# The entropy model of a fused attention kernel in another order: two steps of one side together, and a first tanh over 2048 columns

## The reference

```
# x: (8, 192, 64, 64) float32; gn: group norm over 32 groups
x = x + attention(gn(x))        # q, k: 24 channels, v: 192 channels, each 1x1 conv + prelu; softmax over 4096 positions
x = x + likelihood(gn(x))

def logits_cumulative(logits, ms, bs, fs):            # per channel, widths 1, 3, 3, 3, 1
    for i in range(4):
        logits = einsum('cij,cjn->cin', softplus(ms[i]), logits) + bs[i]
        if i < 3:
            logits = logits + tanh(fs[i]) * tanh(logits)
    return logits
def likelihood(x):
    lower = logits_cumulative(x - 0.5, ...)
    upper = logits_cumulative(x + 0.5, ...)
    sign = -sign(lower + upper)
    return maximum(abs(sigmoid(sign * upper) - sigmoid(sign * lower)), 1e-6)
```

## Time and profile before

| | |
|---|---|
| median of 3 runs | 4760.89 us (4754.21 to 4761.35) |
| the profiled execution's own time | 4754.35 us |
| its span | 4752.5 us |
| PE busy | 4428.2 us, 93% |
| DVE busy | 4099.3 us, 86% |
| ACT busy | 3736.5 us, 79% |
| mean granted TensorE clock | 0.984 |
| DMA, share of 16 engines | 21.4% (the SP queue) |

### The profile page before, as it was taken

How to read it: one execution, slowest core, us unless ns; L and a number is a source line. 1 busy time by engine, 2 the same in 40 slices (tenths; PEclk the granted TensorE clock), 3 DMA queues, 4 the chain that set the end, 5 groups by cost and what they waited for, 6 DMA issues and landing times.

```text
span 4752.5 us, 108300 instructions
## 1 busy us (share of the span) xinstructions
PE 4428.2 (93%) x38780; PEld 2977.4 (63%) x38780; DVE 4099.3 (86%) x5433; ACT 3736.5 (79%) x4214; POOL 813.8 (17%) x937
## 2 busy tenths in 40 slices
PE   5999989999899999999899998999989999899976
PEld 3888338873488735887258862688617885278821
DVE  6997899978999789996999969999698987999866
ACT  2777788868888698886988869787797877978787
POOL 4100201202022110211111120121201212022112
PEclk9999999999999999999999999999999999999998
DMA  2000321114211142111411124110331112311133
GB/s 68 25 21 25 97 73 53 38 39 100 68 51 36 44 103 62 46 44 40 111 51 53 36 58 104 40 61 28 78 89 49 47 41 75 93 49 34 40 93 94
DMA packets 155019, 280.19 MB, mean 59 GB/s; under 512 B 37441, under 2 KB 37921, under 8 KB 152706
## 3 DMA queue, kind: packets, MB, share of 16 engines
q1 hardware_dynamic: 154434, 272.69, 21.4%
HBM read 205.24 MB, written 50.33 MB: 54 GB/s over the span
## 4 chain that ended last, share of the span: by engine, by line
PE 72%; ACT 11%; DVE 7%; issue 7%; DMA 0%; ACTq 0%; POOL 0%; DVEq 0%; POOLq 0%
PE ps L1514 14%; PE ps L1512 14%; PE ps L1516 13%; PE ps L1288 9%; PE ps L1465 8%; ACT th L799 5%; ACT arena L792 4%; PE ps L1387 3%; PE ps L1321 3%; DVE th L1123 3%; PE ps L1373 3%; PE ps L1345 2%; DVE mxp L1191 2%; PE ps L1296 1%; PE ps L1280 1%
## 5 line engine op out<-in xcount | busy, mean ns | idle before, releaser
L1514 PE MATMUL ps<-v_sb,arena 128*128 128x192 f16 x8192 | 2026.8, 247 | 0.0
L1512 PE MATMUL ps<-v_sb,arena 128*128 128x193 f16 x8192 | 2017.9, 246 | 0.0
L1516 PE MATMUL ps<-v_sb,arena 128*128 128x193 f16 x8192 | 2009.9, 245 | 0.0
L755 ACT ACTIVATE arena<-ps 128x1024 f16<-128x1024 f32 x1024 | 1049.0, 1024 | 644.5 <-PE ps L1288 640.7
L1083 DVE TENSOR_TENSOR arena<-ps,arena 128x1024 f16<-128x1024 f32 x1024 | 1245.6, 1217 | 166.8 <-ACT ps L756 158.5
L1191 DVE TENSOR_REDUCE mxp<-ps 128x1 f32<-128x512 f32 x1792 | 1191.0, 688 | 41.3 <-PE ps L1465 29.3
L1123 DVE SCALAR_TENSOR_TENSOR th<-th,gates,ps 128x1024 f32<-128x1024 f32 x768 | 950.3, 1277 | 147.2 <-ACT th L799 140.1
L756 ACT ACTIVATE ps<-ps 128x1024 f32<-128x1024 f32 x1024 | 1044.4, 1020 | 0.0
L1514 PEld LDWEIGHTS ps<-v_sb,arena 128*128 128x128 f16 x8192 | 795.1, 97 | 262.7 <-issue 0.6
L799 ACT ACTIVATE th<-ps,biases 128x1024 f32<-128x1024 f32 x768 | 825.6, 1120 | 118.5 <-PE ps L1373 80.8
L1512 PEld LDWEIGHTS ps<-v_sb,arena 128*128 128x128 f16 x8192 | 792.1, 97 | 126.3 <-issue 10.8
(11 more groups left out here) (147 smaller groups left out, 3449.8 us busy)
## 6 DMA issues: line engine op xcount, KB each, us to landing
x<-x2d SPq DMA_DIRECT2D x1152, 64.0 KB, 2.3
arena<-x2d SPq DMA_DIRECT2D x768, 64.0 KB, 2.5
xp<-x_dram SPq DMA_DIRECT2D x18, 1536.0 KB, 10.1
shared<-x_dram SPq DMA_DIRECT2D x64, 384.0 KB, 3.9
x2d<-shared SPq DMA_DIRECT2D x64, 384.0 KB, 3.0
res<-x2d SPq DMA_DIRECT2D x96, 256.0 KB
out_dram<-res SPq DMA_DIRECT2D x96, 256.0 KB
kst<-shared SPq DMA_DIRECT2D x32, 256.0 KB, 3.2
```

What stands on the lines that cost most here:

```text
L755: act.activation(e_hi[:, q % 4, :].rearrange("p (k n) -> p k n", k=2), sc, ACT.Exp)
L1512: pe.matmul(acc, eh, v_sb[:, m, 0:C + 1], start=(m == 0 and t % 2 == 0), stop=False, skip_group_check=True)
L1514: pe.matmul(acc[:, 0:C], eh, v_sb[:, m, VW:VW + C], start=False, stop=False, skip_group_check=True)
L1516: ins = pe.matmul(acc, el, v_sb[:, m, 0:C + 1], start=False, stop=(m == MT - 1), skip_group_check=True)
```

## The change

Steps are ordered by side. Step c now has side d = c // 2 % 2, so a pair of steps w (HALVES, 24 in an image) is a whole unit's 4096 positions of one side: u = w // 2, d = w % 2. Each engine takes a pair at a time:

- PE: first layer of 2w, one piece of side work, first layer of 2w + 1, third layer of pair w - 1 (one side only, four matmuls and one PSUM bank), second layer of 2w, another piece of side work, second layer of 2w + 1. Side work is value bank V_LEAD + 2w + i, or maximum 2 (w - 6) + i.
- ACT: the two tanh of the first layer, the first tanh of pair w + 2, the two tanh of the second layer, then the Relu of value banks V_LEAD + 2w and + 1.
- DVE: a reduction, the two gates of the first layer, the logits of pair w - 1, a reduction, the two gates of the second layer, then the two value instructions.

The first tanh of a pair is one instruction over 2048 columns (for the first pair it stays in pieces). x4 has two slots of a whole unit; a unit is loaded by six DMAs of 128 KB, and the first two units in halves. The side rows are loaded by two DMAs of 128 KB for a pair. t0 keeps its three tiles, th1 has four, th2 two. The wait of the first tanh is for both halves of its unit. The diff also brings weights w3f and w3h, which would take the second gate over into the third layer's matmuls for steps that are `folded`; FOLD is (False, False), so no step is, and every gate is left to DVE.

```diff
-X4R, T0R, HR1, HR2, XR, LUR = 3, 3, 2, 5, 4, 6
-LEAD = 4
-SPLIT = 1
+X4R, T0R, HR1, HR2, XR, LUR = 2, 3, 4, 2, 4, 6
+X4_DMAS = SIDES * (UNITS // X4R + 1)
+FOLD = (False, False)
...
-FIRST_AT = VB - V_LEAD + 1
+FIRST_AT = (VB - V_LEAD + 1) // 2
...
     uses = []
+    for w in range(HALVES + 1):
+        if w < HALVES:
+            uses += [("h1", 2 * w), ("h1", 2 * w + 1)]
+        if w >= 1:
+            uses.append(("h3", w - 1))
+        if w < HALVES:
+            uses += [("h2", 2 * w), ("h2", 2 * w + 1)]
...
+            def load_side(row, w):
+                for a in (1, 0):
+                    sp.dma_start(t0[64 * a + 48:64 * a + 64, w % T0R, :, :].rearrange("p d (k n) -> p (d k) n", n=N),
+                                 whole(row, w // 2, a)).then_inc(side_in[w % T0R], 16)
...
-                    load_side(l, row, 0)
                     store_x2(l, row, BLOCKS - 1)
                     for s in range(2):
                         sp.wait_ge(x2_stored[s], l * 64 + 64)
-                    load_x4(row, 1)
+                    load_side(row, 0)
+                    for u in range(X4R):
+                        load_half(row, 2 * u + 1)
...
+            pool.memset(w3f[:, :, :], 0.0)
+            pool.memset(w3h[:, :, :], 0.0)
...
+                def first_tanh(w, half=None):
+                    u, d = w // 2, w % 2
+                    if d == 0 and half != 1:
+                        loaded = 2 * SIDES + u // X4R * SIDES
+                        act.wait_ge(x4_in[u % X4R], l * X4_DMAS * 16 + loaded * 16)
+                    if w >= T0R:
+                        act.wait_ge(h1_mm, l * SLOTS + 2 * (w - T0R) + 2)
+                    if half is None:
+                        act.activation(t0[:, w % T0R, :, :], x4[:, u % X4R, :].rearrange("p (d n) -> p d n", d=2),
+                                       ACT.Tanh, bias=biases[:, d, 0, u:u + 1], scale=scl[:, u:u + 1]
+                                       ).then_inc(t0_ready, 2)
...
+                for w in range(HALVES + (0 if proj else 3)):
+                    if w < HALVES:
+                        for c in (2 * w, 2 * w + 1):
+                            if c >= HR1:
+                                act.wait_ge(h3_mm, l * HALVES + w - 1)
+                            tanh("h1", c, th1[:, c % HR1, :, :], 1, h1_mm, t1_ready)
+                    if w + 2 < HALVES:
+                        first_tanh(w + 2)
...
+                    if w < HALVES:
+                        for c in (2 * w, 2 * w + 1):
+                            if c >= HR2:
+                                act.wait_ge(h3_mm, l * HALVES + w)
+                            tanh("h2", c, th2[:, c % HR2, :, :], 2, h2_mm, t2_ready)
...
+                    for i in range(2):
+                        v = V_LEAD + 2 * w + i
+                        if proj and v < VB:
+                            negative(QK + v)
...
+                for w in range(HALVES + (0 if proj else 3)):
+                    m = 2 * (w - FIRST_AT)
+                    if proj and 0 <= m < MAXES:
+                        first_reduce(m)
...
+                    if w < HALVES:
+                        for c in (2 * w, 2 * w + 1):
+                            gate("h1", c, th1[:, c % HR1, :, :], F1O, t1_ready, h1_ready)
+                    if 1 <= w <= HALVES:
+                        logits(l, w - 1, not proj)
+                    if proj and 0 <= m < MAXES:
+                        first_reduce(m + 1)
...
+                            if not folded(c):
+                                gate("h2", c, th2[:, c % HR2, :, :], F2O, t2_ready, h2_ready)
+                    for i in range(2):
+                        v = V_LEAD + 2 * w + i
+                        if proj and v < VB:
+                            value(QK + v)
...
+                def side_work(w, i):
+                    v, m = V_LEAD + 2 * w + i, 2 * (w - FIRST_AT) + i
+                    if proj and v < VB:
+                        value_bank(v)
+                    if proj and 0 <= m < MAXES:
+                        first_max(m)
+                    if proj and m == MAXES + 1:
+                        turn_max(pj(BLOCKS, 0), 0)
+
+                for w in range(HALVES + (0 if proj else 1)):
+                    if w < HALVES:
+                        first_layer(2 * w)
+                        side_work(w, 0)
+                        first_layer(2 * w + 1)
+                    if w >= 1:
+                        third_layer(l, w - 1)
+                    if w < HALVES:
+                        if proj and w == HALVES - 1:
+                            pe.wait_ge(max_in, pj(BLOCKS * 16, 16))
+                            scores(0, 0)
+                        second_layer(2 * w)
+                        side_work(w, 1)
+                        second_layer(2 * w + 1)
```

More of the change, by code:

```diff
@@ L38 @@
 STACK_DMAS = 5
-X4_DMAS = 2 * 3
-SIDE_DMAS = 2 * 2
+SIDES = 2 * 3
+SIDE_DMAS = 2
 NORM_DMAS, CONST_DMAS = 3, 6
@@ L125, in max_tiles, with folded, unfolded_before @@
     return list(range(min(PER_STEP * p, MAXES), min(PER_STEP * (p + 1), MAXES)))
+def folded(c):
+    return FOLD[c // 2 % 2]
+def unfolded_before(c):
+    return sum(not folded(i) for i in range(c))
 def tail_unit(i, last):
@@ L209, in program @@
         w3 = sb("w3", [P, UNITS, 2 * UC])
+        w3f = sb("w3f", [P, UNITS, 2 * UC])
+        w3h = sb("w3h", [P, UNITS, 2 * UC])
         gates = sb("gates", [P, UNITS, NF])
@@ L247, in program @@
         place = [0]
-        second = th2.rearrange("p s d n -> p (s d n)")
+        first = th1.rearrange("p s d n -> p (s d n)")
         def setup_area(*shape):
@@ L481, in phase_b @@
                         sp.wait_ge(x_sums, summed_up)
-                        for v in (0, 2):
-                            load_x4(row, v)
+                        for u in range(X4R):
+                            load_half(row, 2 * u)
                     if j + 1 < BLOCKS:
@@ L573, in coefficients @@
                     spread(w2, i, 1, msp[:, :, M2C + i])
+                setup(pool.tensor_tensor(u1[:, :, 0], msp[:, :, M3C], gates[:, :, F2O], ALU.mult))
+                dot(u1[:, :, 1], [(msp[:, :, M3 + i], msp[:, :, M2C + i]) for i in range(HID)])
                 for a in range(2):
-                    ins = spread(w3, a, 2 + a, msp[:, :, M3C])
+                    spread(w3, a, 2 + a, msp[:, :, M3C])
+                    spread(w3f, a, 2 + a, u1[:, :, 0])
+                    ins = spread(w3h, a, 2 + a, u1[:, :, 1])
                 ins.then_inc(set_gp, 1)
@@ L1188, in phase_b @@
+                if proj:
+                    low(pj(BLOCKS * PAIRS, 0), 0)
             def phase_b(b, l):
```

248 lines of the change are left out of this document (106 added, 142 removed).

## The result

The changed kernel takes 4945.64 us (median of 4 runs, 4934.94 to 4950.15), the one before 4759.53 beside it: 1.039 times as long, interval 1.0371 to 1.0409. The forecast was 4890 us, slower. The direction was right, and the time lies 0.6 us above the top of the range, 4945. The profiled execution took 4934.94 us, with a mean granted clock of 0.972 against 0.984 before; it is the lowest of the four. Against the profiled execution before (4754.35) it is 181 us more, where the sum had 138.

The account below looks back on a forecast made before the run. PE, ACT and DVE were taken as nearly full, so order counts too. Seven images lose 14.6 + 2.6 + 4.3 = 21.5 us each, the last gains 12: 4754 + 138 = 4892, said as 4890; range 4825 to 4945.

Parts of the forecast that it names:

- The ring: Value stage: PE stands at V for the value two banks before; 10.13 us a pair, stage 15.6 us longer.
- rival (c): Faster: ACT's wide tanh carries the value stage, bound by ACT, and DVE the maxima; 4703 us, chance 0.07.
- The clock: PE at half clock behind some of the new stalls: 4.3 us an image, between none and 10.2.
- (a): Rival: each stall of PE brings the low clock, 10.2 us an image; 4934 us, chance 0.15.
- The maxima: Stage with the 32 maxima: 110.6 us against 110.36, so 0.2 us an image lost.
- The new ring: Maxima: chain from reduction through G1a, P2a, second maximum, P2b, T2b, G2b to reduction; 6.82 us a pair against 6.90.
- The last stage: Behind the maxima, to the first product with V: one gate less, 1.2 us an image gained.
- The head: Start of each image: first F 2.3 us late, waiting for both halves, plus Relu delay; 2.6 us an image lost.
- The last image: No banks or maxima, ACT sets the pace: 1.15 us less for each of 12 units; 12 us gained in all.
- The sum: Whole kernel: seven images lose 21.5 us each, the last gains 12; 4754 + 138 = 4892, said as 4890.

Follow-up runs that it names:

- e1: Changed kernel with the first Relu and value instruction of a pair moved between its first and second layer; 4819.22 us, 1.0129 times the kernel before.
- e10: Kernel before the change, with each value bank issued right behind the step's first layer instead of at the step's end; 4958.21 us, 1.0421.
- e7: Changed kernel with the first value bank of pairs 1 to 5 issued ahead of the pair's first first-layer group instead of behind it; 5030.83 us, 1.0574.
- e2: Changed kernel with 22 small extra matmuls on PE ahead of the banks of pairs 1 to 5 and the first maximum; 4913.33 us, 1.033.
- e5: Changed kernel with the first tanh's parts each waiting for their own input half, unit 0's second half issued ahead of side loads; 4902.79 us, 1.03.
- e8: Changed kernel with four edits: value work earlier, second maximum ahead of P2a, separate half semaphores, head Relus in old order; 4763.05 us, 1.0014.
- e3: Changed kernel with the second maximum of a pair issued on PE ahead of P2a instead of between P2a and P2b; 4916.05 us, 1.0333.

## Why the prediction was off in size

**The ring: right.** V is released by DVE's value instruction, PE idles 2.28 us before it (forecast 2.2), and a pair has 10.26 us (10.13). The difference is in three distances between PE's groups, 1.02, 1.00 and 1.01 where the forecast had 0.97, 0.93 and 0.97; for the second it had called the sixteen matmuls of its row eight, but halved their time rightly. e1 takes the wait away and the stage falls by 14.4 us, e10 plants it in the old kernel, e7 makes it longer. Free of the low clock the stage is 60.57 us, 16.1 more than before (15.6 forecast). Of these, 11.7 are the wait; the other 4.4, which e1 keeps, are PE's (a dearer first pair above all), and stood in the ring's terms unseen: rival (c), a stage set by ACT, would have failed without the wait too.

**The clock: right in kind, too high in this stage.** 2.7 us an image there (e2) against 4.3. Of the rivals, (a) asked for all six stalls; one to four spells were seen in an image, in a program that repeats itself. Of the four runs, which span 15 us, the shortest has the highest mean granted clock (0.972) and the longest the lowest (0.968). e10 and e7, with 22 and 23 us an image at half clock, show how near the rival was.

**The maxima: mis-sized.** The sum had 0.2 us and 3.1 were measured. The ring has 6.92 us, not 6.82. From the rows of the changed kernel,

```profile
1206.90 1.27 DVE L1159 SCALAR_TENSOR_TENSOR th<-th,gates,ps 128x1024 f32<-128x1024 f32 x1
...
1208.32 1.09 PE L1445 MATMUL ps<-th,w 64*64 64x512 f32 x8 [0.72 <-DVE th L1159]
1209.34 0.39 PE L1414 MATMUL ps<-kst,qst 128*128 128x512 f16 x1
1209.66 1.09 PE L1445 MATMUL ps<-th,w 64*64 64x512 f32 x8
...
1209.53 1.11 ACT L830 ACTIVATE th<-ps,biases 128x1024 f32<-128x1024 f32 x1
1210.88 2.12 ACT L830 ACTIVATE th<-ps,biases 128x1024 f32<-128x1024 f32 x2 [0.24 <-PE ps L1445]
```

P2b to T2b is 1.22 (1209.66 to 1210.88), not 1.16, and G1a (1206.90) to P2a 1.42, not 1.38: 0.1 us in each of fifteen pairs. Pair 6 was left 5.8 us and takes 7.56 (e2); the reduction and split, at 2.5, add 1.0 to the last pair. With the maxima of e1, where neither a wait nor the half clock enters, the stage is 111.74, 1.65 above before; the M that waits for the last value adds 0.65 (112.39 in e2) and the half clock 0.8. The forecast compared its ring with 110.36, a stage with 3.4 us at half clock, and not with the 109.61 of three others. It also took 110.36 / 16 = 6.90 us for two steps of before, which has the wait of the first M in it. Late in that stage four steps, from gate to gate, took 13.54:

```profile
649.49 2.47 DVE L1123 SCALAR_TENSOR_TENSOR th<-th,gates,ps 128x1024 f32<-128x1024 f32 x2
...
663.03 2.47 DVE L1123 SCALAR_TENSOR_TENSOR th<-th,gates,ps 128x1024 f32<-128x1024 f32 x2
```

That is 6.77 us for two. The new ring, forecast to be 0.08 us shorter than the old pace, is 0.15 longer in each pair.

**The last stage: -0.1 instead of -1.2.** In four images it takes 15.4 to 15.5 us (-0.7), in the three others, with 5 us of it at half clock, 17.0 to 17.1. Where the other 0.5 us of the forecast went in the four is open.

**The head: the step that failed.** The sum had 2.6 us an image, 5.5 were measured. F is 2.6 us late where 2.3 were forecast, but by two errors that nearly cancel: eight issues take 5.03 us (1092.20 to the end of the sixth half at 1097.23) and not 3.6, since the price of a 64 KB issue (0.45) was taken for the side loads of 128 KB, and in this image they begin 3.55 us ahead of the statistics (1095.75), where the row of before has 1067.99 - 1.10 - 1064.45 = 2.44. What was wrong was the rest. Behind F the forecast had 0.85 us for a Relu behind the wide F and some 0.5 us taken back, since DVE and PE waited there anyway. The Relus' place costs about what it was given: 0.7 us, from e5 to e8. But nothing is taken back: a late F costs 1.8 us more than its own lateness (22.58 us from F to the first gate, and 20.79 in e5). PE's wait at the value bank is 2.83 us instead of 1.53, and 6.0 us of the stretch lie at half clock instead of 3.5; how the 1.8 divides between the two, no run shows. Together 0.3 (ahead of the statistics) + 2.6 + 1.8 + 0.7 are the head's 5.5.

**The last image: right in sum, in part by luck.** 11.4 us gained, 12 forecast. One unit has

```profile
4776.40:4790.82 14.42, 10.77 (x84) 2.37 (x80) 11.73 (x11) 14.20 (x14) 3.83 (x4) 1.00 0.77 112
```

14.42 us with ACT busy 14.20, where it had 15.36 and 14.75: 0.94 us less, 1.15 forecast. The earlier trace rows By stages, the head of that image loses 3.8 us (2.2 forecast), the stretch from the first gate to the 45th gains 8.2 (eleven units, 12.7 forecast), and the stretch behind it gains 7.0 (33.9 us before, 26.9 after), where the forecast had one unit's 1.15. That last gain stood in no term, and nothing here explains it.

**The sum.** Per image the terms are off by +2.9 (head), +2.9 (maxima), +1.1 (last stage), +0.5 (ring) and -1.6 (clock): 5.8, times seven 41 us. The profiled execution is besides 10.7 us below the median of its runs, and the one before 5 below its own: from run to run the time moves by as much as a term. The range ended 11 us above rival (a), 4934 us, which has every stall at half clock but no error in the head or the maxima.

## What to carry to other kernels

Where a rotating buffer is freed by the last instruction of the step before, its next use must not stand at the front of an in-order queue: measure the distance from the freeing instruction to the use in the queue, in instructions and not in buffers. One bank placed a few groups sooner, with the same work and the same buffers, cost the old kernel 4%; the freeing instruction moved ahead of two gates gave the new one back 2.5%. When steps are made twice as large, price the start of each stage anew: the first large load has to be issued and landed whole before the first large instruction, and a late start can cost more than its own lateness (2.6 us late, 4.4 us lost).

## What the runs showed of the hardware

- Six DMAs of 128 KB behind one another take 4.23 us of SP's queue, 0.70 each, where those of 64 KB take 0.45 to 0.475; two side loads of 128 KB at the head of the second image held it for 2.18 us. The 128 KB land after 4.8 us (3.8 for side rows) where 64 KB land after 2.3 to 2.6. With fewer and larger DMAs of the same short rows this queue moves 272.6 MB as before, but takes 26.7% of the DMA engines' time instead of 21.4%.
- Stalls of PE of 2.2 to 2.3 us in each pair are now and then followed by a spell at 1.2 GHz, and not by one each; a value stage had from none to five of them (both in e3). Putting 22 matmuls of 1.39 us in all into each stall took every spell of that stage away, and the kernel ran 32 us faster. What decides between one spell and four was not found.
